# In the first layer's attention steps, VectorE takes the low half of the turned probabilities first and the row maximum second

## The reference

```python
scores = jnp.einsum('bqhd,bkd->bhqk', q, k) * scale
scores = jnp.where(causal[None, None], scores, min_val)
attn = jax.nn.softmax(scores, axis=-1)
ctx = jnp.einsum('bhqk,bkd->bqhd', attn, v)
```

## Time and profile before

| | us |
|---|---|
| median of 3 runs | 1162.2 |
| lowest, highest | 1160.69, 1166.45 |
| the profiled execution's own time | 1162.79 |
| its span | 1161.0 |
| TensorE busy | 1071.3 (92%) |
| VectorE busy | 831.8 (72%) |
| ScalarE busy | 689.0 (59%) |
| GpSimd busy | 480.6 (41%) |

### The profile page before, as it was taken

One profiled execution on the slowest core, in us unless ns is written; L12 is line 12 of the kernel. 1 busy time (PEld: TensorE's weight loads), 2 busy tenths in 40 slices (PEclk: granted clock), 3 DMA queues, 4 the chain that ended last, 5 costly groups with the idle time before them and its releaser, 6 DMA issues.

```text
span 1161.0 us, 21474 instructions
## 1 busy us (share of the span) xinstructions
PE 1071.3 (92%) x7506; PEld 982.7 (85%) x7506; DVE 831.8 (72%) x1611; ACT 689.0 (59%) x1916; POOL 480.6 (41%) x544
## 2 busy tenths in 40 slices
PE   4778899989988688999999999999999999999997
PEld 3667788878877677888999999999999999899996
DVE  4677777777775565888777777677777767777775
ACT  3666665666565443555566666666766666555553
POOL 2564554456375100002774434444433434488200
PEclk9899999999999899999999999999999999999999
DMA  7846656664855337662544455454445443233220
GB/s 235 147 146 157 160 169 148 167 206 128 176 180 153 128 104 200 181 221 87 191 128 139 122 168 155 130 151 139 133 133 170 144 131 113 87 108 108 66 98 19
DMA packets 143113, 166.16 MB, mean 143 GB/s; under 512 B 10807, under 2 KB 109112, under 8 KB 142944
## 3 DMA queue, kind: packets, MB, share of 16 engines
q1 hardware_dynamic: 139935, 156.41, 46.8%
q0 software_dynamic: 3072, 8.39, 2.2%
HBM read 116.13 MB, written 48.63 MB: 142 GB/s over the span
## 4 chain that ended last, share of the span: by engine, by line
PE 57%; DVE 11%; DMA 11%; POOL 8%; ACT 5%; SPq 4%; issue 3%; DVEq 0%; POOLq 0%; ACTq 0%
PE ps_m L1644 24%; PE ps_s L1644 10%; DMA scales<-d_scales 7%; PE ps_t L1644 6%; PE ps_b L1644 3%; POOL d_xs L1293 3%; PE ps_c L1644 2%; ACT probs L476 2%; PE ps_t L1760 2%; PE ps_c L1760 2%; PE ps_m L824 2%; SPq L322 1%; DVE neg_max L761 1%; PE ps_b L824 1%; POOL parts L441 1%
## 5 line engine op out<-in xcount | busy, mean ns | idle before, releaser
L1405 ACT ACTIVATE probs_a<-ps_s,neg_max_a 128x256 f32<-128x256 f32 x256 | 118.0, 473 | 144.1 <-DVE neg_max_a L1610 144.1
L1644 PE MATMUL ps_m<-xTa,w_qk 128*128 128x512 f32 x768 | 199.0, 398 | 4.0 <-DVE v L1463 1.6
L1644 PEld LDWEIGHTS ps_m<-xTa,w_qk 128*128 128x128 f32 x768 | 136.9, 188 | 34.2 <-issue 5.4
L476 ACT ACTIVATE probs<-ps_s,neg_max 128x128 f32<-128x128 f32 (+1 forms) x256 | 104.9, 420 | 70.7 <-DVE neg_max L761 69.3
L1610 DVE TENSOR_REDUCE neg_max_a<-ps_s 128x2 f32<-128x512 f32 x128 | 88.1, 691 | 51.9 <-PE ps_s L1644 50.2
L1306 POOL CAST we_down<-raw_down_e 88x512 fp32r<-88x512 f32 x47 | 28.6, 609 | 217.9 <-DMA raw_down_e<-in_we_down 217.9
L1644 PE MATMUL ps_m<-w_v,xTa 128*128 128x256 f32 x768 | 106.2, 288 | 0.0
L1644 PE MATMUL ps_t<-pTa,v 128*128 128x256 f32 x768 | 103.5, 284 | 0.0
L1644 PE MATMUL ps_s<-kTa,qTa 128*128 128x256 f32 x768 | 102.9, 283 | 0.3 <-DVE kTa L1441 0.2
L486 ACT ACTIVATE pT<-ps_t 128x512 fp32r<-128x512 f32 x96 | 57.7, 602 | 67.5 <-PE ps_t L889 66.6
L1644 PEld LDWEIGHTS ps_s<-kTa,qTa 128*128 128x128 f32 x768 | 96.7, 191 | 1.0 <-DVE kTa L1441 0.7
(11 more groups left out here) (248 smaller groups left out, 2783.6 us busy)
## 6 DMA issues: line engine op xcount, KB each, us to landing
w_qk<-d_w_head SPq DMA_DIRECT2D x64, 512.0 KB, 3.9
raw_up<-in_we_up SPq DMA_DIRECT2D x47, 352.0 KB, 3.5
d_w_head<-parts SPq DMA_DIRECT2D x128, 128.0 KB, 2.2
raw_down_e<-in_we_down SPq DMA_DIRECT2D x47, 176.0 KB
codes<-in_w_codes SPq DMA_DIRECT2D x64, 128.0 KB
scales<-d_scales SPq DMA_DIRECT2D x64, 128.0 KB
q<-d_q_scr SPq DMA_DIRECT2D x24, 256.0 KB, 6.7
d_xs<-zeros SPq DMA_DIRECT2D x16, 384.0 KB, 7.7
```

The costliest lines, as they stand in the source:

```text
L476: last = act.activation(probs[:, g % 3, a * w:(a + 1) * w], ps_s[g % 2][:, a * w:(a + 1) * w], ACT.Exp, bias=neg_max[:, g % 2, a:a + 1], s ...
L1405: last = act.activation(probs[:, s, t, :], ps_s[s][:, t * SEQ:(t + 1) * SEQ], ACT.Exp, bias=neg_max[:, s, t:t + 1], scale=1.0, accum_out=s ...
L1644: last = pe.matmul(out, lhs[i], rhs[j], start=start and n == 0, stop=stop and n == 2, skip_group_check=True)
```

## The change

In VectorE's `step(g)` the two instructions of the pair change places. Nothing else is touched: no semaphore, no buffer, no other engine's order, and the number of instructions stays.

```diff
@@ -755,15 +755,15 @@
                     dve.tensor_scalar(w[:], raw[:], ZERO_POINT, None, ALU.subtract).then_inc(gate_up_ready, 1)
             early_item(item)
         def step(g):
+            if 2 <= g < ALL + 2:
+                dve.wait_ge(t_high.sem, t_high.at(0, g - 1))
+                dve.tensor_tensor(pT[1][:, g % 2, :], ps_t[:], pT[0][:, g % 2, :].bitcast(F32), ALU.subtract)\
+                    .then_inc(t_low.sem, 1)
             if g < ALL:
                 nh = DC * units[g][4]
                 dve.wait_ge(s_full.sem, s_full.at(0, g + 1))
                 dve.tensor_reduce(neg_max[:, g % 2, 0:nh], ps_s[g % 2][:].rearrange("p (h k) -> p h k", h=nh), AX.X,
                                   ALU.max, negate=True).then_inc(max_ok.sem, 1)
-            if 2 <= g < ALL + 2:
-                dve.wait_ge(t_high.sem, t_high.at(0, g - 1))
-                dve.tensor_tensor(pT[1][:, g % 2, :], ps_t[:], pT[0][:, g % 2, :].bitcast(F32), ALU.subtract)\
-                    .then_inc(t_low.sem, 1)
             for item in late[g - 1] if g else ():
                 if item[0] == "out":
                     residual_sum(item)
```

## The result

The changed kernel takes 1201.85 us (median of 4 runs, 1200.53 to 1204.46), the kernel before 1161.45 in the same comparison: ratio 1.034, interval 1.031 to 1.037, or 40 us more. Forecast were 30 us more and 1193, with a range of 1172 to 1214. The profiled execution took 1203.04 us with a span of 1201.3.

What follows compares the result with a forecast made beforehand. TensorE was taken as the fullest engine, the maximum as what others wait for. Stretches +21.5 to 34.2 us plus last light steps 2 to 3 gave 23.5 to 37.2; middle +30 on 1162.79 made 1193, range 1172 to 1214.

Steps and rivals of the forecast that it cites:

- The ring: Layer one's steps: copy, low half, maximum, exponentials, items, next copy run in sequence; ScalarE stands still some 1.35 us every step.
- The gain: Where VectorE comes late to a pair, the low half starts up to 0.61 us earlier, saving TensorE at most 12.8 us.
- The sum over stretches: Steps 2 to 89 in seven stretches: +21.5 us if steps even out fully, +39.9 if nothing does.
- The cover late in turn 3: VectorE's 5.34 us wait for a store hides the loss of steps 66 to 89, 0 to 5.7 us.
- the last light steps: Steps 91 to 94 of layer one, light again, add 2 to 3 us.
- Turn 0: Layer one's first turn: to end some 10 us later, with +7 us that nothing more can hide.
- my two ways: Per-step sums for steps 2 to 94, over ScalarE and over VectorE; the longer counts: light 2.85, heavy 6.9 us.
- the clock, which I had as a rival: Turn 0 runs at 0.50 clock throughout: +26 us on top, 1219 us; chance 0.03.
- More is hidden: Rival: layer one hides more than counted; turn 0's +7 and a third of the rest remain, about +12, 1175 us; chance 0.12.
- faster: Rival: ScalarE's idle time swallows the exponentials' delays, only earlier turnings count: -12.8, 1150 us; chance 0.03.
- nothing evens out: Rival: layer one's steps do not even out and the weight chunks move along: +59, 1222 us; chance 0.08.

Runs made afterwards that it cites:

- the wait without the place: Kernel before with the maximum still first but also waiting for ScalarE's copy (t_high): ratio 1.010 to the kernel before.
- the ten late steps alone: Kernel before with the new order only in ten steps where VectorE came late to the pair: ratio 1.004 to the kernel before.
- the fillers: Changed kernel plus eight and twelve matmuls with unused results in two of TensorE's waits in turn 0: ratio 1.033 to the kernel before.
- turn 0 alone: Kernel before with the new order only in steps 0 to 23: ratio 1.014 to the kernel before.
- ScalarE's new order: Changed kernel with ScalarE doing copy, the step's items, then exponentials ahead of the late items: ratio 0.998 to the kernel before.

## Why the prediction was right, and what it missed

- **The ring.** Right, in the numbers that it rests on: the exponentials begin at least 1.35 us behind the copy's end in 94 of 94 steps (median 1.36; before, 0.48), two light low halves lie 2.86 us apart, the heavy step takes 6.9 us. That the loss hangs on it is shown from both sides: the wait without the place costs 9 to 16 us, and with the items taken out of the ring on ScalarE the change costs 12 to 16 us and not 40. What is left then fits the light steps, where no item can fill the wait, and the clock; that part was not tested by itself.
- **The gain.** Forecast was at most 12.8 of TensorE's 13.5 us, and that the light steps would eat it. It is now 15.4 us in 17 waits: none came. With the ten late steps alone it fell by 3.3 us, and layer one still ended later.
- **The sum over stretches.** For the seven stretches I had bounds of +4.9 to 9.1, 3.5 to 6.9, 7.0 to 8.2, 0.2 to 2.9, 5.9 to 7.1, 0 to 2.2, 0 to 3.5. Measured: +15.7, 4.5, 5.2, 5.0, 6.1, 2.3, 3.7, sum 42.6, which is over even the upper sum of 39.9. Four lie in their bounds or within 0.2 us of them; the first is far over, the fourth over, the third under. These are the ways between the turnings of units 1, 17, 31, 41, 55, 65, 79 and 89, as the prediction's own times of now were, and those stand in steps 3, 19 and so on, a step later than its headings say. Cut at the turnings of the steps that it names, the first stretch takes 51.1 us before, its bounds become +8.1 to 12.3, and it is still over them at +15.7; the others shift by up to 3 us to either side. So the total tells more than the single stretches, and it was ten short.
- **The cover late in turn 3.** Half right. The wait for the store shrank from 5.34 to 2.61 us, and the way from the turning of unit 89 to that of 90, 13.9 us before, became 2.6 shorter; I had let it swallow all of up to 5.7. The four ways behind it grew by 0.8 us, where 2 to 3 were forecast for the last light steps.
- **What was mis-sized.** Turn 0 first: it was to end some 10 us later and ends 18.6 later. Two terms were at nothing. TensorE's own waits for items within a step were not in my two ways: L569, gated_s and sT grew by 20 us together. And the clock, which I had as a rival with 3 in 100, for all of turn 0, while the sum has TensorE's busy time stay as it was. It did not stay. Layer one and the stage behind it, before:

```profile
38.20:408.20 370.00, 322.40 (x2194) 287.77 (x2193) 263.11 (x526) 226.99 (x750) 185.85 (x235) 0.96 0.59 159
408.20:1161.00 752.80, 729.55 (x5233) 680.23 (x5231) 549.67 (x1042) 447.69 (x1145) 285.27 (x291) 1.00 0.43 132
```

and layer one now:

```profile
38.70:450.20 411.50, 335.94 (x2195) 298.83 (x2194) 262.46 (x526) 223.53 (x750) 184.71 (x235) 0.94 0.53 143
```

Of the 41.5 us more, 28.0 are idle time of TensorE (47.6 to 75.6) and 13.5 are busy time, for the same matmuls, at 0.94 granted and not 0.96. The two pieces of turn 0 account for 4.4 of the 13.5. How much of the rest is clock can be read from the stretches at 0.50: there are four in layer one before (in us, 41.4 to 48.2, 65.3 to 68.7, 140.4 to 147.2, 382.7 to 393.0) and eleven now, five of them in turn 0. Their sums, before and now:

```profile
sum 27.30, PE 22.30 PEld 20.35 DVE 14.28 ACT 13.14 POOL 8.65; mean PE 5.57 PEld 5.09 DVE 3.57 ACT 3.29 POOL 2.16
...
sum 47.60, PE 46.66 PEld 43.97 DVE 21.22 ACT 22.44 POOL 20.42; mean PE 4.24 PEld 4.00 DVE 1.93 ACT 2.04 POOL 1.86
```

TensorE was busy at the low clock for 46.7 us and not 22.3. Work that takes 2.76 us there takes 1.60 at the high one, so that, by my estimate from these rows, 20 us went to the low clock and not 9: some 10 of the 13.5. That each of them also lengthened layer one is not shown; the fillers say that some of it would have been waited away. Without the 4.4 of the two pieces the first stretch would be at +11.3, still over its bound of 9.1.
- **Rivals.** "More is hidden" and "faster" fell in turn 0 alone, which lost 17.9 us. Of "nothing evens out", +59, the truth is two thirds. (The range ends at +51, 1214 us, and not at the +53 that stands with this rival.)
- **On 1.2 GHz.** The changed kernel's stretch at 0.65 follows a wait of 1.72 us behind a turning that itself ran with little else, and in the kernel before the stretch from 60 to 70 us, with TensorE's wait of 2.9 us for the low half in it, had 0.83 (row above). But the wait does not tell it alone. In the changed kernel with ScalarE's new order, TensorE waited only 0.48 us at that place, and the clock fell all the same, to 0.60 over the piece:

```profile
81.73 0.54 PE L961 MATMUL ps_m<-ident,rinv_wide 128*128 128x128 f32 x2 [0.48 <-ACT rinv_wide L567]
...
85.65 2.76 PE L972 MATMUL ps_m<-w_down,hT 128*128 128x256 f32 x12
```

Nor does the busy time just ahead: over the ten us before the piece it was 6.8 us in the changed kernel, and 6.3 in the kernel with the wait alone, whose piece ran at 1.00. What decides here stays open. The rule of the Trainium skill ("TensorE: Matmul & The Clock Gate", Part 1: The HAM clock gate), that an idle array falls to half its clock, agrees in direction: with 28.0 us more of idle time the stretches at half clock grew from 27.3 to 47.6 us.

## What to carry to other kernels

When two instructions on one engine each feed another, ask what the other engine does between them: here the low half waits for ScalarE and the maximum is what ScalarE waits for, and in the order "wait for it, then feed it" the two engines take turns (1.36 us from the copy to the exponentials, 94 times) where they had worked side by side. That the first is ready a little earlier pays for nothing of this. The same question, asked of the other engine's queue, gave a real gain of 14 us: put what is wanted at once (the items) ahead of what is wanted two steps later (the exponentials). And where two changes are combined, hold the pair against each alone: the kernel with both came out level with the one before, and yet the change on VectorE still cost it 12 us.

## What was not expected of the hardware

A wait of 1.72 us and the short turning ahead of it were followed by half clock for most of the next 28 matmuls: L972's twelve took 2.76 us, and 1.60 with fillers in the wait; and they took 2.76 too where the wait was 0.48 us. Over layer one the stretches at half clock went from four to eleven. And two chips were some 30 us slower than the others in the stage behind layer one (782 to 788 us against 751 to 755) with layer one alike, so that kernels of two chips can't be compared by their times. Part of it is one place: in the trace of the kernel with the wait alone, TensorE was busy for 4.85 of the 20 us from 580 on, at 0.50 granted. Why is not shown.
